# A planner's durations for GpSimd's indirect DMAs, and the order of work made anew from them

## Chip, cores and metric

The kernel runs on one core of one Trainium2 chip. The metric is the device time of one execution in microseconds, as the median of several runs. Lower is better.

## What is computed

Eight sequences of 512 tokens with 128 features pass through two macaron layers: a half-weighted mixture of experts, an attention, and the same half-weighted mixture again.

```python
x = x + 0.5 * _L0_ffn_ref(_layernorm(x, axis=-1), ...)   # 24 experts, hidden 512, top 2
x = x + _L0_attn_ref(_layernorm(x, axis=-1), ...)        # linear attention, 16 heads
x = x + 0.5 * _L0_ffn_ref(_layernorm(x, axis=-1), ...)
x = x + 0.5 * _L1_ffn_ref(_layernorm(x, axis=-1), ...)   # 8 experts, hidden 256, top 2, and a shared one
x = x + _L1_attn_ref(_layernorm(x, axis=-1), ...)        # causal attention with rotary positions
x = x + 0.5 * _L1_ffn_ref(_layernorm(x, axis=-1), ...)
```

Each mixture picks the two best experts of each token from its router's scores and adds their outputs, weighted.

## The kernel before

**Streams and rounds.** The eight sequences ("batches") are two streams `s` of four batches `b` each. There are four rounds `p` of experts: rounds 0 and 1 with the 24 experts of layer L0, rounds 2 and 3 with the 8 experts of L1. The linear attention lies at the start of round 1 and the causal attention at the start of round 3. `p` = 4 is the last combination and the store. While one stream is with its experts, the other is in routing and attention.

**The way of a round.** A batch is normalised (`norm_g`), turned into rows of two halves (`send_g`), and scored (`score`). When the batches of a part are scored, VectorE picks the experts (`r_top`), counts (`r_rank`, with a matmul on TensorE), and works out where each token's row goes (`r_slot`, lines 2216 to 2262, the last instruction of which is the cast of line 2259 that writes `slot_index`). GpSimd then writes the rows to DRAM by expert, the *scatter* (line 2520): 16 indirect DMAs for one part of a round, two batches by four tiles of 128 tokens by two choices. SyncE fetches the rows back transposed (`fetch`, line 2636). TensorE runs the experts (`l1`, lines 1711 to 1713, and `l2`, lines 1737 to 1750), ScalarE and VectorE serve them (`hid`, lines 1957 and 2065), and SyncE stores the outputs to DRAM (`ystore`, line 2649). GpSimd brings each token's two outputs back, the *gather* (line 2540): 8 indirect DMAs a batch. VectorE adds them to `x_res` (`add`, line 2332), and the next round begins. There are 16 scatters and 32 gathers, so 256 + 256 indirect DMAs.

**What sets the order.** Each engine works through its own list in order, and an instruction that waits holds back all behind it. The lists are made by `Plan` when the program is built. It is a simulation by events with a duration for each step (`work`, line 234). Whenever an engine comes free in it, `dispatch` (line 467) gives it the waiting step of lowest rank. The rank starts with 2p + s, to which `EARLIER` (line 920) adds a number by engine, kind and round in `rank_on` (line 926). A negative number puts a step ahead, a positive one back, and 2 is the distance of one round. The rank of a step of the experts on ScalarE or VectorE that has no number there is shifted by `FIRST` = -10. GpSimd has no number at all. Its list follows the rank 2p + s alone among the scatters and gathers that are ready at that moment. A scatter or a gather is not interrupted.

**Pace.** The plan's times are used once more, in `paces` (line 356). For each pair of indirect DMAs of GpSimd it looks for the last step of TensorE that has ended in the plan when that pair starts, and `keep_pace` (line 2489) makes GpSimd wait for the semaphore of this step. Before a scatter GpSimd also waits for `slot_index`, before a gather for the stores of the outputs.

Of the kernel before, what the change touches and what calls it, by code (L numbers as in the profile page):

```python
# [232 lines left out]

def work(ev):


# [680 lines left out]

EARLIER = {(SC, "bias"): 0, (SC, "ca_flip"): -1, (SC, "ca_score"): -3, (SC, "ca_v"): 3, (SC, "gates_1"): -1, (SC, "hid", 0): 0, (SC, "hid", 1): -1, (SC, "l1"): -2, (SC, "l1", 0): -1, (SC, "l1", 1): 1, (SC, "l1", 2): -1, (SC, "l1", 3): -3, (SC, "la_qk"): -3, (SC, "la_soft"): -4, (SC, "la_vg"): 3, (SC, "late_split"): -4, (SC, "norm_a"): -0.5, (SC, "norm_g", 1): 1, (SC, "norm_g", 2): 0.5, (SC, "norm_g", 3): -0.5, (SC, "r_gap"): -3, (SC, "r_gap", 1): -1, (SC, "r_soft"): 0.5, (SC, "r_soft", 2): 3, (SC, "r_soft", 3): -1, (SC, "send_a"): 2, (SC, "send_g", 1): -0.5, (SC, "send_g", 3): 2, (SC, "shared1"): -3, (SC, "shared1", 3): -0.5, (SC, "split_0"): -0.5, (SC, "split_1"): 0.5, (SC, "turn_a"): 0.5, (SC, "turn_g"): -4, (SC, "ystore"): -0.5, (SC, "ystore", 0): 1, (SC, "ystore", 2): 0.5, (PE, "ca_flip"): -1, (PE, "ca_out"): -1, (PE, "ca_q"): 0.5, (PE, "ca_score"): 2, (PE, "ca_v"): 1, (PE, "halve_0"): 2, (PE, "la_heads"): -2, (PE, "la_mix"): 0.5, (PE, "la_out"): -2, (PE, "la_qk"): -0.5, (PE, "la_vg"): -0.5, (PE, "r_end", 0): -3, (PE, "r_end", 1): -3, (PE, "r_rank"): 1, (PE, "r_rank", 0): -3, (PE, "r_rank", 1): -3, (PE, "r_rank", 2): 3, (PE, "r_rank", 3): 2, (PE, "score"): -0.5, (PE, "score", 1): 2, (PE, "score", 2): 2, (PE, "shared1"): 1, (PE, "shared2"): -4, (PE, "shared2", 3): -1, (PE, "split_0"): -3, (PE, "turn_a"): -3, (VE, "add"): 3, (VE, "add", 1): 2, (VE, "add", 2): 0.5, (VE, "bias"): 0, (VE, "ca_flip"): 0.5, (VE, "ca_k"): -3, (VE, "ca_out"): -3, (VE, "ca_score"): -3, (VE, "empties"): 2, (VE, "hid"): 0, (VE, "hid", 0): -4, (VE, "hid", 1): -3, (VE, "la_heads"): 0.5, (VE, "la_mix"): 1, (VE, "la_second"): 1, (VE, "la_soft"): -2, (VE, "norm_a", 1): -0.5, (VE, "norm_g"): -3, (VE, "norm_g", 0): 1, (VE, "norm_g", 3): -1, (VE, "r_end", 0): 3, (VE, "r_end", 2): -1, (VE, "r_end", 3): -4, (VE, "r_gap", 0): -2, (VE, "r_gap", 1): 1, (VE, "r_norm", 2): 3, (VE, "r_page", 1): 3, (VE, "r_rank"): -4, (VE, "r_rank", 0): -0.5, (VE, "r_rank", 2): -4, (VE, "r_rank", 3): 0.5, (VE, "r_send"): 3, (VE, "r_send", 1): -1, (VE, "r_share"): -1, (VE, "r_share", 1): -0.5, (VE, "r_share", 2): 3, (VE, "r_share", 3): 3, (VE, "r_slot"): -3, (VE, "r_slot", 0): 0, (VE, "r_slot", 1): 2, (VE, "r_slot", 2): 0.5, (VE, "r_soft", 3): -1, (VE, "r_top"): 1, (VE, "r_top", 0): 0.5, (VE, "r_top", 2): -1, (VE, "score"): 0.5, (VE, "score", 1): -0.5, (VE, "score", 2): 1, (VE, "score", 3): 3, (VE, "send_a"): 0, (VE, "send_g", 1): -1, (VE, "send_g", 3): 3, (VE, "shared2", 2): 2, (VE, "split_1"): -0.5}  # L920
# [1877 lines left out]
```

How the kernel before makes its waits and increments, by code:

```python
    def wait_ge(self, signal, value):  # L962
        if self.passed.get(signal, 0) < value:
            self.passed[signal] = value
            self.do.wait_ge(signal.sem, value)
# [352 lines left out]
        def second_ready(lane, layer):  # L1318
            n = LAYERS.index(layer)
            if layer.terms:
                lane.wait_ge(*w2_low.after_all(w2_halves[n]))
            else:
                lane.wait_ge(second_loaded[n], 16 * layer.chunks)
# [80 lines left out]
        def before_set(lane, ev, b):  # L1405
            pool, user = plan.sets_for(ev.p), Ev("set", ev.s, ev.p, b)
            old = pool.before[user]
            if old:
                for read in set_read(old):
                    lane.wait_ge(*read)
            elif pool.at[user] == START_SET:
                lane.wait_ge(*w1_low.after_all(w1_splits[0] + w1_splits[1]))
                for layer in LAYERS:
                    if layer.terms:
                        second_ready(lane, layer)
                for s, zeroed in enumerate(rows_zeroed):
                    lane.wait_ge(zeroed, 16 * len(ZERO_PARTS[s]))
            else:
                lane.wait_ge(block_parked, 16 * len(pieces[L1]))
# [11 lines left out]
        def gates_ready(lane, ev):  # L1431
            sent = turn_of("g", *ev[1:])
            lane.wait_ge(*w1_low.after(split_of(GATE_PART)))
            lane.wait_ge(*xt_landed[plan.xt.at[sent]].after(sent))
# [15 lines left out]
            def bank_free(ev, j=0):  # L1451
                old = plan.banks.before[ev, j]
                if old:
                    t.wait_ge(*bank_read(*old))
```

## Time and profile before

| what | value |
|---|---|
| median of 3 runs | 1012.48 us (1011.15 to 1014.36) |
| the profiled execution | 1013.01 us |
| its span, first to last instruction | 1011.7 us |
| mean granted clock of TensorE | 0.913 of full speed |
| busy: TensorE matmuls | 818.3 us, 81% |
| busy: VectorE | 658.2 us, 65% |
| busy: ScalarE | 640.2 us, 63% |
| busy: GpSimd (POOL) | 498.4 us, 49% |

The shares are averages over stages with different limits. GpSimd's busy time leaves out the 0.3 us that stand between two of its DMAs in a row, and which the views put down as "issue". TensorE's matmuls overlap, and a busy TensorE is not one at its peak.

### The profile page before, as it was taken

How to read it: one execution, taken by the hardware profiler on the slowest of the kernel's cores; microseconds unless marked ns; L12 is line 12 of the kernel's file. 1: busy time of each engine (PE TensorE's matmuls, PEld its weight loads, DVE VectorE, ACT ScalarE, POOL GpSimd, SP SyncE). 2: the span in 40 equal slices, each digit the busy share in tenths (PEclk: the TensorE clock that was granted, in tenths of full speed). 3: DMA queues.
4: the chain of work that ended last, by engine and by line, in shares of the span. 5: the costliest groups of instructions: out<-in, count | busy, mean ns of one | idle time of the engine just before them, and what ended most of it. 6: DMA issues, size and time to landing. Idle time of an engine off the chain costs nothing.

```text
span 1011.7 us, 25625 instructions
## 1 busy us (share of the span) xinstructions
PE 818.3 (81%) x9531; PEld 701.5 (69%) x9531; DVE 658.2 (65%) x2266; ACT 640.2 (63%) x1200; POOL 498.4 (49%) x519
## 2 busy tenths in 40 slices
PE   5897999998983486989898898865788979897940
PEld 3446899977883255888887798752777858686840
DVE  5986875495884784898377852588567858673022
ACT  5476789879883376888787874543566657463420
POOL 0272650370007771026374277777536637376775
PEclk9998999999997687999999999867799989998985
DMA  8888864552425124585466468542664454466852
GB/s 281 296 258 246 233 142 115 112 122 60 78 51 121 52 74 87 110 198 119 119 138 115 78 143 219 120 110 63 120 134 91 102 112 105 112 146 129 173 154 75
DMA packets 254167, 134.32 MB, mean 133 GB/s; under 512 B 171936, under 2 KB 232288, under 8 KB 254048
## 3 DMA queue, kind: packets, MB, share of 16 engines
q1 hardware_dynamic: 237664, 99.11, 42.8%
q0 software_dynamic: 16384, 33.59, 12.0%
q8 instruction: 80, 1.31, 0.6%
q14 instruction: 39, 0.32, 0.1%
HBM read 40.09 MB, written 56.89 MB: 96 GB/s over the span
## 4 chain that ended last, share of the span: by engine, by line
PE 26%; DVE 11%; POOL 8%; DMA 7%; issue 5%; ACT 4%; SPq 1%; ACTq 0%; POOLq 0%; DVEq 0%
POOL got L2540 5%; PE bank L1740 5%; POOL rows L2520 3%; PE bank L1711 3%; PE bank L1713 3%; PE bank L1712 3%; DMA got<-y_l,slot_index 2%; PE bank L1529 2%; DVE hid L2065 2%; SPq L2636 1%; DMA turned<-rows 1%; PE bank L1631 1%; PE bank L1653 1%; DMA rows<-rows_sent,slot_index 1%; PE bank L1746 1%
## 5 line engine op out<-in xcount | busy, mean ns | idle before, releaser
L2520 POOL DMA_INDIRECT rows<-rows_sent,slot_index x192 | 189.2, 985 | 303.5 <-issue 189.5
L2540 POOL DMA_INDIRECT got<-y_l,slot_index x256 | 245.6, 959 | 172.7 <-issue 68.0
L1711 PE MATMUL bank<-turned,first_high_l 128*128 128x128 f16 x1248 | 233.1, 225 | 54.2 <-DMA turned<-rows 37.3
L1712 PE MATMUL bank<-turned,first_high_l 128*128 128x128 f16 x1248 | 232.8, 224 | 0.0
L1713 PE MATMUL bank<-turned,first_low_l 128*128 128x128 f16 x1248 | 232.6, 224 | 0.0
L2065 DVE SCALAR_TENSOR_TENSOR hid<-bank,hid 128x512 f16<-128x512 f32 x220 | 145.1, 685 | 83.9 <-ACT hid L1957 82.5
L1711 PEld LDWEIGHTS bank<-turned,first_high_l 128*128 x1248 | 125.9, 101 | 64.6 <-issue 63.5
L1950 ACT ACTIVATE bank<-bank 128x512 f32<-128x512 f32 x220 | 128.0, 588 | 58.4 <-PE bank L1713 54.1
L2332 DVE SCALAR_TENSOR_TENSOR x_res<-got,share,x_res 128x128 f32<-128x128 f32 x256 | 77.6, 348 | 121.9 <-DMA got<-y_l,slot_index 119.5
L1957 ACT ACTIVATE hid<-bank 128x512 f16<-128x512 f32 x220 | 127.9, 597 | 9.3 <-PE bank L1750 5.4
L1712 PEld LDWEIGHTS bank<-turned,first_high_l 128*128 x1248 | 125.9, 101 | 4.0 <-issue 2.3
L1713 PEld LDWEIGHTS bank<-turned,first_low_l 128*128 x1248 | 126.0, 101 | 0.0
L1746 PE MATMUL bank<-second_low_l,hid 128*128 x880 | 122.7, 220 | 0.0
L1745 PE MATMUL bank<-second_high_l,hid 128*128 x880 | 122.7, 220 | 0.0
L1740 PE MATMUL bank<-second_l,hid 128*128 x736 | 115.7, 297 | 0.0
L1740 PEld LDWEIGHTS bank<-second_l,hid 128*128 128x128 f32 x736 | 101.4, 200 | 2.6 <-issue 0.6
L1968 ACT ACTIVATE y<-bank 128x512 f32<-128x512 f32 x104 | 60.9, 585 | 66.9 <-DMA y_l<-y 30.4
L1737 PE MATMUL bank<-bias,select_l 128*128 128x128 f16 x404 | 89.7, 222 | 4.5 <-ACT hid L1950 3.7
L1824 ACT ACTIVATE xn<-x_res,norm 128x128 f32<-128x128 f32 x136 | 56.0, 486 | 56.5 <-DVE norm L2103 56.4
L1745 PEld LDWEIGHTS bank<-second_high_l,hid 128*128 128x128 f16 x880 | 86.4, 98 | 2.6 <-issue 2.3
L1750 PE MATMUL bank<-second_high_l,hid 128*128 x880 | 85.6, 220 | 2.4 <-DVE hid L2065 2.4
L1746 PEld LDWEIGHTS bank<-second_low_l,hid 128*128 128x128 f16 x880 | 86.5, 98 | 0.0
(304 smaller groups left out, 1660.4 us busy)
## 6 DMA issues: line engine op xcount, KB each, us to landing
y_l<-y SPq DMA_DIRECT2D x92, 256.0 KB
rows<-own SPq DMA_DIRECT2D x14, 512.0 KB, 5.9
got<-in_w_dram SPq DMA_DIRECT2D x27, 256.0 KB, 5.0
hid<-in_w_dram SPq DMA_DIRECT2D x25, 256.0 KB, 3.9
got<-y_l,slot_index POOLq DMA_INDIRECT x256
rows<-rows_sent,slot_index POOLq DMA_INDIRECT x192, 2.2
y_l<-y SPq DMA_DIRECT2D x12, 192.0 KB
x_res<-in_x_dram SPq DMA_DIRECT2D x8, 256.0 KB, 4.8
```

Source lines behind the costliest of these rows:

```text
L1711: t.do.matmul(out, cut_of(high[c], e), xh, start=True, stop=False)
L1712: t.do.matmul(out, cut_of(high[c], e), xl, start=False, stop=False)
L1713: m = t.do.matmul(out, cut_of(low[c], e), xh, start=False, stop=True)
L1737: t.do.matmul(out, spread(select[layer][:, bass.ds(e, 1)]), bcol("b2_0" if layer is L0 else "b2_1"), start=True, stop=False)
L1740: m = t.do.matmul(out, hid[:, j * H + c * P:j * H + c * P + P], cut_of(seconds[layer][0][c], e), start=False, stop=(c == C - 1))
L1745: t.do.matmul(out, upper, cut_of(high[c], e), start=False, stop=False)
L1746: t.do.matmul(out, upper, cut_of(low[c], e), start=False, stop=False)
L1950: a.do.activation(out, hb, ACT.Gelu, scale=1 / (X_SCALE * W_SCALE)).then_inc(hidden_gelu[ev.s].sem, 1)
L1957: m = a.do.activation(hid[:, 0:n], bank_of(l1)[:, 0:n], ACT.Copy, scale=HID_SCALE)
L2065: m = v.do.scalar_tensor_tensor(hid[:, SEQ:SEQ + n], bank_of(l1)[:, 0:n], HID_SCALE, hid[:, 0:n], ALU.mult, ALU.subtract)
L2520: d = g.do.indirect_dma_start(rows_dram[s], at, rows[:, 2 * D * i:2 * D * i + 2 * D], None)
L2540: d = g.do.indirect_dma_start(got_mem[slot][:, col:col + D], None, y_dram[layer][s][layer.team(ev.i)], at)
```

## The change

Two durations of `work` are raised, those of the scatter and the gather. `EARLIER` is replaced as a whole. Nothing else is edited: no instruction is added or taken away, and what follows is another order of the instructions in the engines' lists and other steps for GpSimd to wait for. `EARLIER` is one line of some 150 entries. Here it stands with the entries of which the text speaks, one group to a line.

```diff
-        "scatter": [[(GP, 1.0 * TOP_K * tokens, 2.2)]], "gather": [[(GP, 1.0 * TOP_K * BT, 2.4)]], "add": [[(VE, 3.0, 0.1)]],
+        "scatter": [[(GP, 1.265 * TOP_K * tokens, 2.2)]], "gather": [[(GP, 1.23 * TOP_K * BT, 2.4)]], "add": [[(VE, 3.0, 0.1)]],
...
-EARLIER = {
-  (SC, "hid", 0): 0, (SC, "hid", 1): -1, (SC, "ystore"): -0.5, (SC, "ystore", 0): 1, (SC, "ystore", 2): 0.5,
-  (PE, "score"): -0.5, (PE, "score", 1): 2, (PE, "score", 2): 2,
-  (VE, "add"): 3, (VE, "add", 1): 2, (VE, "add", 2): 0.5,
-  (VE, "hid"): 0, (VE, "hid", 0): -4, (VE, "hid", 1): -3,
-  (VE, "norm_g"): -3, (VE, "norm_g", 0): 1, (VE, "norm_g", 3): -1,
-  (VE, "r_top"): 1, (VE, "r_top", 0): 0.5, (VE, "r_top", 2): -1,
+EARLIER = {
+  (SC, "hid"): 1, (SC, "hid", 0): 0.5, (SC, "ystore", 0): 2, (SC, "ystore", 1): 1, (SC, "ystore", 2): 0.5,
+  (PE, "score"): 0, (PE, "score", 2): -4,
+  (VE, "add", 1): -2, (VE, "add", 2): -1, (VE, "add", 3): 0.5,
+  (VE, "hid", 0): -2,
+  (VE, "norm_g"): 3, (VE, "norm_g", 0): -2, (VE, "norm_g", 2): -1, (VE, "norm_g", 3): -0.5,
+  (VE, "r_top"): -2, (VE, "r_top", 0): -0.5, (VE, "r_top", 1): -1, (VE, "r_top", 3): -1,
...
```

## Rows read from the trace of the kernel before

**Rows 1.** Page, busy us, share of the span, number of instructions of TensorE and GpSimd

```profile
PE 818.3 (81%) x9531; PEld 701.5 (69%) x9531; DVE 658.2 (65%) x2266; ACT 640.2 (63%) x1200; POOL 498.4 (49%) x519
```

**Rows 2.** Page, the chain that ended last, its shares of the span by line

```profile
POOL got L2540 5%; PE bank L1740 5%; POOL rows L2520 3%; PE bank L1711 3%; PE bank L1713 3%; PE bank L1712 3%; DMA got<-y_l,slot_index 2%; PE bank L1529 2%; DVE hid L2065 2%; SPq L2636 1%; DMA turned<-rows 1%; PE bank L1631 1%; PE bank L1653 1%; DMA rows<-rows_sent,slot_index 1%; PE bank L1746 1%
```

**Rows 3.** Windows: stretch, its length, busy us (instructions) by engine, clock, DMA, GB/s

```profile
302.00:385.00 83.00, 43.85 (x337) 31.57 (x337) 57.19 (x208) 41.26 (x69) 63.48 (x64) 0.75 0.31 78
...
574.00:717.00 143.00, 110.87 (x1214) 95.99 (x1214) 84.41 (x332) 71.53 (x138) 108.53 (x112) 0.84 0.56 132
...
881.00:1007.00 126.00, 82.03 (x919) 76.86 (x918) 43.91 (x179) 44.55 (x86) 92.05 (x96) 0.86 0.59 135
...
970.00:980.00 10.00, 3.15 (x29) 2.90 (x27) 2.46 (x8) 1.09 (x2) 7.56 (x9) 0.91 0.47 131
```

**Rows 4.** Groups by line on GpSimd, with busy us, mean ns, idle before, releasers

```profile
L2540 POOL DMA_INDIRECT got<-y_l,slot_index x256 | 245.6, 959 | 172.7 <-issue 68.0 <-PE bank L1750 35.8 <-PE bank L1500 18.3
L2520 POOL DMA_INDIRECT rows<-rows_sent,slot_index x192 | 189.2, 985 | 303.5 <-issue 189.5 <-PE bank L1713 45.9 <-PE bank L1462 40.5
```

**Rows 5.** GpSimd in order of time: start, us, instruction, idle before and its releaser

```profile
362.91 0.94 POOL L2540 DMA_INDIRECT got<-y_l,slot_index  x1 [0.31 <-issue]
364.16 1.00 POOL L2520 DMA_INDIRECT rows<-rows_sent,slot_index  x1 [0.30 <-issue]
...
686.22 1.00 POOL L2520 DMA_INDIRECT rows<-rows_sent,slot_index  x1 [0.30 <-issue]
...
844.96 1.00 POOL L2520 DMA_INDIRECT rows<-rows_sent,slot_sent  x1 [0.30 <-issue]
...
901.11 1.00 POOL L2520 DMA_INDIRECT rows<-rows_sent,slot_index  x1 [0.30 <-issue]
```

**Rows 6.** Chain that ended last, pieces of four scatters: start, us, what

```profile
372.65 0.96 POOL rows L2520
373.91 0.96 POOL rows L2520
...
704.23 0.95 POOL rows L2520
...
862.03 0.96 POOL rows L2520
...
911.64 0.95 POOL rows L2520
```

**Rows 7.** VectorE in order of time, the last cast of four `r_slot`

```profile
357.08 0.40 DVE L2259 CAST slot_index<-route_l 128x8 int32<-128x8 f32 x1
...
679.32 0.17 DVE L2259 CAST slot_index<-route_l 128x8 int32<-128x8 f32 x1
...
835.29 0.16 DVE L2259 CAST slot_index<-route_l 128x8 int32<-128x8 f32 x1
...
896.40 0.17 DVE L2259 CAST slot_index<-route_l 128x8 int32<-128x8 f32 x1
```

**Rows 8.** Waits over the span: who waited for whom, us, times, longest

```profile
DVE x_res L2332 <- DMA got<-y_l,slot_index: 119.5, 28, 31.5
```

**Rows 9.** VectorE in order of time around 330 us

```profile
329.79 1.26 DVE L2332 SCALAR_TENSOR_TENSOR x_res<-got,share,x_res 128x128 f32<-128x128 f32 x4 [6.60 <-DMA got<-y_l,slot_index]
334.75 1.26 DVE L2332 SCALAR_TENSOR_TENSOR x_res<-got,share,x_res 128x128 f32<-128x128 f32 x4 [3.70 <-DMA got<-y_l,slot_index]
335.94 0.25 DVE L2139 TENSOR_SCALAR scores<-bank 128x96 f32<-128x96 f32 x1
```

**Rows 10.** GpSimd in order of time, two waits for TensorE

```profile
471.32 0.96 POOL L2520 DMA_INDIRECT rows<-rows_sent,slot_index  x1 [2.98 <-PE bank L1713]
...
931.25 0.96 POOL L2520 DMA_INDIRECT rows<-rows_sent,slot_sent  x1 [4.21 <-PE bank L1713]
```

**Rows 11.** GpSimd and VectorE in order of time around 305 us

```profile
304.95 1.71 POOL L2520 DMA_INDIRECT rows<-rows_sent,slot_index  x1 [0.30 <-issue]
...
304.83 1.12 DVE L2370 SCALAR_TENSOR_TENSOR first_high_l<-first_low_l,set_small,first_low_l 128x512 f32<-128x512 f32 x1
```

More of the change, by code:

```diff
@@ L916 @@
 EXPERT_STAGES = ("regs", "fetch", "l1", "hid", "l2", "ystore")
-EARLIER = {(SC, "bias"): 0, (SC, "ca_flip"): -1, (SC, "ca_score"): -3, (SC, "ca_v"): 3, (SC, "gates_1"): -1, (SC, "hid", 0): 0, (SC, "hid", 1): -1, (SC, "l1"): -2, (SC, "l1", 0): -1, (SC, "l1", 1): 1, (SC, "l1", 2): -1, (SC, "l1", 3): -3, (SC, "la_qk"): -3, (SC, "la_soft"): -4, (SC, "la_vg"): 3, (SC, "late_split"): -4, (SC, "norm_a"): -0.5, (SC, "norm_g", 1): 1, (SC, "norm_g", 2): 0.5, (SC, "norm_g", 3): -0.5, (SC, "r_gap"): -3, (SC, "r_gap", 1): -1, (SC, "r_soft"): 0.5, (SC, "r_soft", 2): 3, (SC, "r_soft", 3): -1, (SC, "send_a"): 2, (SC, "send_g", 1): -0.5, (SC, "send_g", 3): 2, (SC, "shared1"): -3, (SC, "shared1", 3): -0.5, (SC, "split_0"): -0.5, (SC, "split_1"): 0.5, (SC, "turn_a"): 0.5, (SC, "turn_g"): -4, (SC, "ystore"): -0.5, (SC, "ystore", 0): 1, (SC, "ystore", 2): 0.5, (PE, "ca_flip"): -1, (PE, "ca_out"): -1, (PE, "ca_q"): 0.5, (PE, "ca_score"): 2, (PE, "ca_v"): 1, (PE, "halve_0"): 2, (PE, "la_heads"): -2, (PE, "la_mix"): 0.5, (PE, "la_out"): -2, (PE, "la_qk"): -0.5, (PE, "la_vg"): -0.5, (PE, "r_end", 0): -3, (PE, "r_end", 1): -3, (PE, "r_rank"): 1, (PE, "r_rank", 0): -3, (PE, "r_rank", 1): -3, (PE, "r_rank", 2): 3, (PE, "r_rank", 3): 2, (PE, "score"): -0.5, (PE, "score", 1): 2, (PE, "score", 2): 2, (PE, "shared1"): 1, (PE, "shared2"): -4, (PE, "shared2", 3): -1, (PE, "split_0"): -3, (PE, "turn_a"): -3, (VE, "add"): 3, (VE, "add", 1): 2, (VE, "add", 2): 0.5, (VE, "bias"): 0, (VE, "ca_flip"): 0.5, (VE, "ca_k"): -3, (VE, "ca_out"): -3, (VE, "ca_score"): -3, (VE, "empties"): 2, (VE, "hid"): 0, (VE, "hid", 0): -4, (VE, "hid", 1): -3, (VE, "la_heads"): 0.5, (VE, "la_mix"): 1, (VE, "la_second"): 1, (VE, "la_soft"): -2, (VE, "norm_a", 1): -0.5, (VE, "norm_g"): -3, (VE, "norm_g", 0): 1, (VE, "norm_g", 3): -1, (VE, "r_end", 0): 3, (VE, "r_end", 2): -1, (VE, "r_end", 3): -4, (VE, "r_gap", 0): -2, (VE, "r_gap", 1): 1, (VE, "r_norm", 2): 3, (VE, "r_page", 1): 3, (VE, "r_rank"): -4, (VE, "r_rank", 0): -0.5, (VE, "r_rank", 2): -4, (VE, "r_rank", 3): 0.5, (VE, "r_send"): 3, (VE, "r_send", 1): -1, (VE, "r_share"): -1, (VE, "r_share", 1): -0.5, (VE, "r_share", 2): 3, (VE, "r_share", 3): 3, (VE, "r_slot"): -3, (VE, "r_slot", 0): 0, (VE, "r_slot", 1): 2, (VE, "r_slot", 2): 0.5, (VE, "r_soft", 3): -1, (VE, "r_top"): 1, (VE, "r_top", 0): 0.5, (VE, "r_top", 2): -1, (VE, "score"): 0.5, (VE, "score", 1): -0.5, (VE, "score", 2): 1, (VE, "score", 3): 3, (VE, "send_a"): 0, (VE, "send_g", 1): -1, (VE, "send_g", 3): 3, (VE, "shared2", 2): 2, (VE, "split_1"): -0.5}
@@ new lines @@
+EARLIER = {(SC, "ca_flip"): -3, (SC, "ca_score"): 1, (SC, "gates_1"): 3, (SC, "halve_0"): 2, (SC, "hid"): 1, (SC, "hid", 0): 0.5, (SC, "l1"): 1, (SC, "l1", 1): -1, (SC, "l1", 3): 2, (SC, "la_qk"): -0.5, (SC, "la_vg"): 3, (SC, "late_split"): -4, (SC, "norm_a"): 2, (SC, "norm_a", 1): 2, (SC, "norm_a", 3): -4, (SC, "norm_g"): 2, (SC, "norm_g", 1): 2, (SC, "norm_g", 2): 2, (SC, "norm_g", 3): 1, (SC, "r_gap"): -4, (SC, "r_soft", 3): -2, (SC, "send_a"): 1, (SC, "send_g"): -4, (SC, "send_g", 1): 3, (SC, "send_g", 2): -1, (SC, "send_g", 3): 1, (SC, "shared1"): 3, (SC, "shared1", 3): -4, (SC, "split_0"): -4, (SC, "turn_g"): -4, (SC, "ystore", 0): 2, (SC, "ystore", 1): 1, (SC, "ystore", 2): 0.5, (PE, "ca_out"): 0.5, (PE, "ca_q"): -0.5, (PE, "halve_0"): 2, (PE, "la_heads"): -3, (PE, "la_out"): -2, (PE, "r_end"): 2, (PE, "r_end", 0): -3, (PE, "r_end", 2): 1, (PE, "r_rank"): -2, (PE, "r_rank", 0): -2, (PE, "r_rank", 1): -0.5, (PE, "r_rank", 2): 0, (PE, "r_rank", 3): 1, (PE, "score"): 0, (PE, "score", 2): -4, (PE, "shared1"): 1, (PE, "shared1", 2): 1, (PE, "shared2", 3): -1, (PE, "split_1"): 0, (PE, "turn_a"): 2, (VE, "add", 1): -2, (VE, "add", 2): -1, (VE, "add", 3): 0.5, (VE, "ca_flip"): -2, (VE, "ca_k"): -2, (VE, "ca_out"): 1, (VE, "ca_score"): -3, (VE, "gates_1"): 0.5, (VE, "hid", 0): -2, (VE, "la_heads"): -2, (VE, "la_mix"): -0.5, (VE, "la_second"): -0.5, (VE, "la_soft"): -2, (VE, "late_split"): 0, (VE, "norm_a"): -0.5, (VE, "norm_a", 1): -1, (VE, "norm_a", 3): 3, (VE, "norm_g"): 3, (VE, "norm_g", 0): -2, (VE, "norm_g", 2): -1, (VE, "norm_g", 3): -0.5, (VE, "r_end", 1): 2, (VE, "r_end", 2): 0, (VE, "r_end", 3): 1, (VE, "r_gap"): -4, (VE, "r_gap", 0): -3, (VE, "r_gap", 1): -3, (VE, "r_norm"): -3, (VE, "r_norm", 2): 1, (VE, "r_page", 1): 3, (VE, "r_rank"): -3, (VE, "r_rank", 3): -3, (VE, "r_send", 1): -0.5, (VE, "r_send", 2): 2, (VE, "r_send", 3): 0, (VE, "r_share", 0): 1, (VE, "r_share", 2): 2, (VE, "r_share", 3): 3, (VE, "r_slot", 0): -0.5, (VE, "r_slot", 1): 2, (VE, "r_slot", 2): 1, (VE, "r_soft"): 0.5, (VE, "r_top"): -2, (VE, "r_top", 0): -0.5, (VE, "r_top", 1): -1, (VE, "r_top", 3): -1, (VE, "score", 2): 2, (VE, "score", 3): -0.5, (VE, "selects"): 1, (VE, "send_a"): 0, (VE, "send_g"): 2, (VE, "send_g", 1): -4, (VE, "send_g", 3): -2, (VE, "shared2", 2): -1, (VE, "shared2", 3): -1, (VE, "split_0"): -4, (VE, "turn_g"): 3}
```

## The prediction

> **What bounds the kernel now.** I read the page first. TensorE is busy for 81% of the span and GpSimd for 49% [rows 1], so neither is the bound everywhere. In the chain that ended last the two lines of GpSimd's indirect DMAs together have 8% and no line of TensorE more than 5% [rows 2]. The chain goes from engine to engine, and the order in the lists decides much of its length. The windows then show where GpSimd is the bound. In three blocks it runs without a pause: 64 DMAs in 83 us, 112 in 143 us and 96 in 126 us, while TensorE is busy for 44, 111 and 82 us and its mean clock lies at 0.75, 0.84 and 0.86 of full speed [rows 3]. So 272 of the 512 DMAs run where GpSimd is saturated, and TensorE is idle there for 39 + 32 + 44 = 115 us.
>
> Next I read the pitch. An indirect DMA counts 959 or 985 ns of busy time [rows 4], but the next one starts 1.26 us later in a scatter [rows 6] and 1.25 us later in a gather [rows 5], as 0.3 us of "issue" stand between them. The plan counted 1.0 us. The new figures, 1.265 and 1.23, are right within 2%. The old plan saw the blocks as 64, 112 and 96 us, some 20% too short, and believed GpSimd free where it was not.
>
> **The change, part by part.** *Durations.* No DMA becomes shorter: 512 instructions at the same pitch, 0 us. What changes is which step stands where. By the new figures a scatter counts 16 x 1.265 = 20.2 us instead of 16, a gather 8 x 1.23 = 9.8 instead of 8.
>
> *GpSimd's list.* A scatter releases a round of experts, so how long it stands ready and isn't started can be read. `r_slot`'s last cast ends at 357.48, 679.49, 835.45 and 896.57 [rows 7]. The scatters that need it start at 364.16, 686.22, 844.96 and 901.11 [rows 5]. In each case a gather stands in front, and the delays are 6.7, 6.7, 9.5 and 4.5 us, together 27.4 us. All four scatters have pieces in the chain that ended last [rows 6], so the delay is on the path. It is the gain if every scatter goes first. But a gather that is overtaken lands a whole scatter, 20.2 us, later, and its batch is the start of the next round. How many of the four are turned round can't be read from the diff, since GpSimd's list has no number of its own and comes out of when the steps are ready in the plan. I take half, 13.7 us, with 0 and 27.4 as the ends.
>
> *VectorE's list.* In all it waits 119.5 us for gathered rows [rows 8]. Where it waits, others stand behind it. Around 330 us the two halves of an `add` wait 6.60 and 3.70 us, and a `score` comes directly behind [rows 9], on which `r_top`, `r_rank`, `r_slot` and the late scatter at 364 depend. In the plan an `add` enters the list only when its gather has landed, and with 8 us for a gather it was put in too early. With 9.8 us it goes behind what is ready. Against this, the new numbers put `add` of round 1 four places forward (2 to -2) and that of round 3 from 3 to 0.5. The most to be had at this place is what the `score` could be earlier, 335.94 - 329.79 = 6.2 us [rows 9]. It pays only if the scatter behind it can use it, so it is largely the same time as the 6.7 us above. I count 0, and 6 as the upper bound.
>
> *The tail.* TensorE is busy for only 3.15 us between 970 and 980 [rows 3] and ends there. At 1006.5 GpSimd's last DMA ends, some 30 us later. The 16 gathers of the last team (two batches) need the last outputs: 16 x 1.25 = 20 us. So up to 10 us of backlog could go if the gathers of the teams that end earlier are done by then. This too is earned only if the third block begins earlier. I count 0 and put 8 into the lower end.
>
> *ScalarE's and TensorE's lists.* `hid` and `ystore` on ScalarE go back by 0.5 to 2 places, `hid` on VectorE in rounds 0 and 1 goes from -4 and -3 to -2 and -10, `score` of round 2 on TensorE from 2 to -4, `norm_g` of round 1 on VectorE from -3 to 3. I see no single wait in the trace that these remove. As a whole they are the orders that suit the new durations. I count 0 with 4 us on either side: no row excludes a gain or a loss, and 4 us is the size of the single waits in rows 9 and 10.
>
> *Pace.* A change in the plan's durations also moves the steps of TensorE that GpSimd waits for. In the old plan pair n of a gather or scatter stood at 2.0 n, now at 2.46 n or 2.53 n, and at the end of a block of 48 pairs the step named stands over 22 us later in the plan. Before, GpSimd was slower than the plan, so the step was mostly long past (0.30 us of idle [rows 5]). The two waits of size were 2.98 and 4.21 us [rows 10]. Now this cushion is gone, and if TensorE is late against the plan, GpSimd is held with all that stands behind it. I take 2 us, between 0 and the price of the third rival below.
>
> *DMA length.* At 304.95 one DMA takes 1.71 instead of 0.96 us, while VectorE works for 1.12 us on a gate with both inputs in SBUF [rows 11]. Against the usual 0.94 to 0.96 us, the means [rows 4] leave at most 8 us over all 512 DMAs, and another order moves a fraction of that: 0, within 2 either way. The Trainium skill (SBUF — State Buffer, Who interferes with whom) says that VectorE and GpSimd lock each other out of a shared pair of ports, and that an instruction of VectorE with two SBUF inputs contends with GpSimd's reads. The trace agrees at this place.
>
> *Sum.* 13.7 - 2 = 11.7 us less. The profiled execution took 1013.01 us (span 1011.7 and 1.3 around it), half a microsecond above the median of 1012.48. From the profiled execution the sum gives 1001.3 and from the median 1000.8. **I predict 1001 us.**
>
> One rule speaks against the new durations. The Trainium skill (DMA: Bandwidth & Descriptors, Latency and other measured facts) puts the first-byte latency of a DMA that GpSimd issues at about 1 us, and calls it the overhead of making the descriptors. If that were the pitch, the old 1.0 would be right, and the new plan would count 512 x 0.25 = 128 us too much on GpSimd. The trace decides otherwise.
>
> **The rivals.** *First: the order is nearly worth nothing* (1010 to 1015). Every scatter pulled forward delays a gather, and both streams meet at the end. For it: the gathers are in the chain more than the scatters [rows 2], so a delayed gather costs as well. Against it: TensorE is idle for 115 us in the blocks [rows 3], so the present exchange isn't balanced. Time: 13.7 gained and 13.7 lost, 1012.
>
> *Second: a larger gain* (below 990). All four scatters start at once (27.4) and the shorter third block takes part of the backlog (8): 1012.5 - 35.4 = 977. For it: the plan erred by 20% on the engine that was saturated in a third of the span. Against it: the four exchanges influence one another, and later blocks shift.
>
> *Third, slower: the pace.* In the three blocks the clock stood at 0.75, 0.84 and 0.86 [rows 3]. With the busy times of 44, 111 and 82 us, TensorE lost 44 x 0.25 + 111 x 0.16 + 82 x 0.14 = 40 us there against full clock. If the plan counts TensorE's steps at full clock, GpSimd now waits for steps that come late, where it had 14 to 24 us of cushion (20% of each block). If a third of the 40 us is passed on and the order brings nothing, the time is 1012.5 + 13 = 1025. It decides from the point where TensorE's lag in a block is larger than what the scatters gain, 13.7 us. For it: the 4.21 us at 931 [rows 10] lie in a scatter of the third block, right on the path. Against it: the clock is low where TensorE waits for GpSimd, so its steps are few there and mostly done in time.
>
> *Fourth: the new plan is right by itself but the chip's other errors grow* (transposes, stores, the queue of SyncE), which a new order meets anew. It works like the third with a smaller price and is counted with it.
>
> **How the numbers follow.** The forecast's case, 990 to 1009: 0.45. The second rival: 0.16. The first: 0.14. The third and fourth: 0.25. A difference of over 0.3% (3 us) is about what a measurement of this kernel can tell from no change. Faster by more is 0.45 + 0.16, and with the edge of the first rival 0.62. Within it 0.12, slower 0.26. The range reaches from 983 (the second rival without its last 6 us) to 1023 (the third nearly whole). The forecast's own range is 990 to 1009.
>
> **What would show it.** Right: GpSimd's scatters start within 2 us of the last cast of `r_slot`, VectorE's waits for gathered rows fall well below 119.5 us, and GpSimd's three blocks begin earlier or are broken up. GpSimd's busy time must stay at 498 us within 3 us. For the third rival: GpSimd's idle time before its DMAs shows waits for TensorE of 2 us and more inside the blocks. For the first: the delays at the scatters are gone, but as much idle time of VectorE or TensorE stands before the adds. Wrong altogether would be a gain or loss before 300 us, where GpSimd is not saturated: then the orders on ScalarE, VectorE and TensorE decide, and the durations are only the occasion.

## The result, and the profile after

The changed kernel takes 963.97 us (median of 4 runs, 960.89 to 970.6), the kernel before 1012.35 beside it. The ratio is 0.953, with an interval of 0.948 to 0.958: 4.7% faster, where I had forecast 1.1%. The direction was right. The time lies outside both ranges that I had given (990 to 1009, and 983 to 1023 with the rivals). The profiled execution took 960.89 us, with a span of 959.5.

The page first: its busy line, two of the lines in 40 slices (tenths busy on GpSimd, tenths of full clock on TensorE), the chain that ended last, and the groups of GpSimd's two kinds of DMA.

```profile
span 959.5 us, 25612 instructions
...
PE 810.3 (84%) x9531; PEld 689.7 (72%) x9531; DVE 659.8 (69%) x2266; ACT 638.6 (67%) x1200; POOL 495.6 (52%) x519
...
POOL 0076441173003777042557077777764675577775
PEclk9898999999998686899999999997999999999985
...
PE 15%; DVE 10%; POOL 7%; DMA 5%; issue 5%; ACT 3%; SPq 0%; ACTq 0%; POOLq 0%; DVEq 0%
POOL got L2540 4%; PE bank L1740 4%; POOL rows L2520 3%; PE bank L1529 2%; DMA xt<-rows_sent 2%; DMA got<-y_l,slot_index 2%; PE bank L1711 1%; DVE x_res L2332 1%; PE bank L1713 1%; PE bank L1712 1%; DVE norm L2078 1%; PE bank L1631 1%; DMA turned<-rows 1%; PE bank L1653 1%; DVE x_res L2415 1%
```

```profile
L2540 POOL DMA_INDIRECT got<-y_l,slot_index x256 | 245.6, 959 | 230.4 <-PE bank L1610 73.1
L2520 POOL DMA_INDIRECT rows<-rows_sent,slot_index x192 | 187.4, 976 | 199.9 <-issue 110.6
```

No engine is given less to do: GpSimd is busy for 495.6 us (498.4 in [rows 1]), and its DMAs take 959 and 976 ns (959 and 985 in [rows 4]). The chain is as mixed as before, with the two lines of GpSimd at 7% in place of 8% [rows 2]. So most of the 52 us lie between the instructions.

To see where, I cut each span at the last `ystore` of each expert stage. TensorE's work is then nearly the same on either side of a cut, apart from some 50 matmuls. VectorE's is not, as the second cut shows below. These are the second, third and last two stretches of before (start and end, length, busy us and instructions of PE, PEld, DVE, ACT and POOL, clock, DMA share, GB/s):

```profile
184.30:311.30 127.00, 116.87 (x1572) 104.35 (x1569) 93.88 (x282) 106.92 (x194) 37.59 (x39) 0.97 0.43 91
311.30:498.40 187.10, 134.53 (x1714) 116.30 (x1715) 128.68 (x415) 119.70 (x214) 87.32 (x90) 0.86 0.47 106
...
931.00:974.00 43.00, 39.47 (x470) 38.23 (x467) 4.95 (x16) 19.54 (x36) 32.63 (x34) 1.00 0.82 184
974.00:1011.70 37.70, 0.00 (x0) 0.00 (x0) 9.83 (x32) 0.49 (x1) 24.58 (x26) 0.56 0.33 88
```

And the same four of after:

```profile
180.50:296.80 116.30, 111.82 (x1554) 99.51 (x1551) 75.42 (x206) 101.04 (x184) 30.46 (x32) 1.00 0.40 88
296.80:482.10 185.30, 146.44 (x1774) 123.80 (x1775) 149.54 (x493) 127.50 (x228) 92.86 (x96) 0.85 0.50 114
...
876.10:922.80 46.70, 42.86 (x506) 42.00 (x506) 5.55 (x19) 20.21 (x36) 35.42 (x38) 0.96 0.87 197
922.80:959.50 36.70, 0.00 (x0) 0.00 (x0) 9.20 (x30) 0.49 (x1) 23.88 (x26) 0.55 0.32 88
```

The same reading for all eleven stretches, where idle is the length less TensorE's busy time:

| stretch ends with | length before | after | TensorE idle before | after |
|---|---|---|---|---|
| round 0, stream 0 | 184.3 | 180.5 | 23.6 | 22.2 |
| round 0, stream 1 | 127.0 | 116.3 | 10.1 | 4.5 |
| round 1, stream 0 | 187.1 | 185.3 | 52.6 | 38.9 |
| round 1, stream 1 | 106.6 | 100.1 | 8.7 | 6.0 |
| round 2, stream 0 | 60.1 | 55.0 | 7.6 | 7.2 |
| round 2, stream 1, first team | 93.3 | 87.4 | 27.1 | 21.2 |
| round 2, stream 1, second team | 52.5 | 46.0 | 2.9 | 1.3 |
| round 3, stream 0, first team | 61.6 | 56.4 | 9.8 | 4.5 |
| round 3, stream 0, second team | 58.5 | 49.1 | 9.9 | 3.0 |
| round 3, stream 1 | 43.0 | 46.7 | 3.5 | 3.8 |
| tail | 37.7 | 36.7 | 37.7 | 36.7 |

TensorE's idle time falls from 193 to 149 us, which is 44 of the 52 us. The other 8 are shorter busy time (818.3 to 810.3), beside a mean granted clock over the span of 0.931 in place of 0.913. There is no one place. Nine stretches give 2 to 11 us each, the last expert stage gives 4 back and the tail gives 1. 14.5 us are there by the second cut (311.3 against 296.8), and in that stretch of before GpSimd is busy for 38 of 127 us. Not all of the 14.5 us is won there. By this cut TensorE is 7 us short of its work of before (51 matmuls) and VectorE 19 us, and the third stretch makes it up: it is hardly shorter, but holds 12 us more of TensorE and 21 us more of VectorE. What is won by the second cut is TensorE's idle time, 33.7 us before and 26.7 after.

What GpSimd does is seen best in order of time, around its first block (start, us, instruction, idle before it and its releaser):

```profile
300.50 0.94 POOL L2540 DMA_INDIRECT got<-y_l,slot_index  x1 [73.08 <-PE bank L1610]
...
304.94 0.94 POOL L2540 DMA_INDIRECT got<-y_l,slot_index  x1 [2.25 <-PE bank L1602]
...
329.45 0.95 POOL L2540 DMA_INDIRECT got<-y_l,slot_index  x1 [2.12 <-PE bank L1557]
...
333.20 0.95 POOL L2540 DMA_INDIRECT got<-y_l,slot_index  x1 [0.30 <-issue]
334.45 1.49 POOL L2520 DMA_INDIRECT rows<-rows_sent,slot_index  x1 [0.30 <-issue]
...
364.29 0.95 POOL L2540 DMA_INDIRECT got<-y_l,slot_index  x1 [0.30 <-issue]
365.54 1.08 POOL L2520 DMA_INDIRECT rows<-rows_sent,slot_index  x1 [0.30 <-issue]
```

The last casts of `r_slot` ahead of these two scatters, and of two more, in VectorE's order of time:

```profile
325.67 0.41 DVE L2259 CAST slot_index<-route_l 128x8 int32<-128x8 f32 x1
...
359.31 0.17 DVE L2259 CAST slot_index<-route_l 128x8 int32<-128x8 f32 x1
...
650.97 0.17 DVE L2259 CAST slot_index<-route_l 128x8 int32<-128x8 f32 x1
...
850.04 0.17 DVE L2259 CAST slot_index<-route_l 128x8 int32<-128x8 f32 x1
```

```profile
654.07 1.00 POOL L2520 DMA_INDIRECT rows<-rows_sent,slot_index  x1 [0.30 <-issue]
...
852.81 1.00 POOL L2520 DMA_INDIRECT rows<-rows_sent,slot_index  x1 [0.30 <-issue]
```

Scatters still stand ready behind gathers. The one at 334.45 waits 8.4 us from the end of its cast (326.08). The four of [rows 5] and [rows 7] go from 6.7, 6.7, 9.5 and 4.5 us to 6.1, 2.9, 1.2 and 2.6. But summed over all sixteen scatters the time from the last cast of `r_slot` to the first DMA is 66.1 us before and 66.2 after. Of this 23.8 and 30.2 us lie in round 0, where there is no gather to stand behind, so rounds 1 to 3 have 42.3 and 36.0. What moved is when they are ready: the casts of [rows 7] at 679 and 896 stand at 651 and 850. So less waiting gives at most 6 us; for the rest, everything ahead of the scatters is earlier.

Which pairs were turned round needs no trace: `Plan`, run on either kernel, gives the lists. Among the 48 scatters and gathers of GpSimd two places differ. The first scatter of round 1 (stream 0) stands behind three gathers of stream 1 and no longer ahead of them. In round 2 the two scatters of stream 1 each pass one gather. Of the four pairs of [rows 5] only one is turned round by this, that of the scatter at 686 (6.7 to 2.9 us). The other three stand behind the same gather as before. The other lists differ far more: TensorE's at 616 of 941 places, ScalarE's at 554 of 885, VectorE's at 472 of 631. The first DMA of GpSimd at which its list differs is this one of before, so up to 302 us the two kernels have the same order on GpSimd:

```profile
302.30 1.00 POOL L2520 DMA_INDIRECT rows<-rows_sent,slot_index  x1 [72.95 <-issue]
```

Waits of after over the span (who waited for whom, us, times, longest):

```profile
DVE x_res L2332 <- DMA got<-y_l,slot_index: 87.7, 22, 29.4
...
PE bank L1711 <- DMA turned<-rows: 5.5, 3, 2.9
```

VectorE waits 87.7 us for gathered rows instead of 119.5 [rows 8]. TensorE waits 5.5 us for rows turned by a transfer. Before this line read:

```profile
PE bank L1711 <- DMA turned<-rows: 37.3, 6, 13.3
```

### The profile page after: what moved, and what is told of

The parts are those of the page before. It is cut to its first block and busy times, and to the rows that moved or that the text cites. A ratio compares the mean times of both kernels' runs of the same rounds, so it can differ in the third digit from the quotient of the medians.

```text
span 959.5 us, 25612 instructions
## 1 busy us (share of the span) xinstructions
PE 810.3 (84%) x9531; PEld 689.7 (72%) x9531; DVE 659.8 (69%) x2266; ACT 638.6 (67%) x1200; POOL 495.6 (52%) x519
## 5 line engine op out<-in xcount | busy, mean ns | idle before, releaser
L1711 PE MATMUL bank<-turned,first_high_l 128*128 128x128 f16 x1248 | 224.8, 220 | 23.9 <-DVE hid L2065 9.1
L1712 PE MATMUL bank<-turned,first_high_l 128*128 128x128 f16 x1248 | 224.4, 220 | 0.0
L1713 PE MATMUL bank<-turned,first_low_l 128*128 128x128 f16 x1248 | 224.3, 220 | 0.0
L1711 PEld LDWEIGHTS bank<-turned,first_high_l 128*128 x1248 | 122.9, 99 | 32.6 <-issue 32.0
L2332 DVE SCALAR_TENSOR_TENSOR x_res<-got,share,x_res 128x128 f32<-128x128 f32 x256 | 77.1, 348 | 94.8 <-DMA got<-y_l,slot_index 87.7
L1712 PEld LDWEIGHTS bank<-turned,first_high_l 128*128 x1248 | 122.9, 98 | 2.1 <-issue 1.0
L1713 PEld LDWEIGHTS bank<-turned,first_low_l 128*128 x1248 | 122.8, 98 | 0.0
L1740 PE MATMUL bank<-second_l,hid 128*128 x736 | 112.4, 291 | 0.0
L1740 PEld LDWEIGHTS bank<-second_l,hid 128*128 128x128 f32 x736 | 98.4, 195 | 2.4 <-issue 0.3
L1950 ACT ACTIVATE hid<-bank 128x512 f32<-128x512 f32 x96 | 53.9, 581 | 54.6 <-PE bank L1713 52.7
```

Of the source, the lines that this page charges most:

```text
L1711: t.do.matmul(out, cut_of(high[c], e), xh, start=True, stop=False)
L1712: t.do.matmul(out, cut_of(high[c], e), xl, start=False, stop=False)
L1713: m = t.do.matmul(out, cut_of(low[c], e), xh, start=False, stop=True)
L1740: m = t.do.matmul(out, hid[:, j * H + c * P:j * H + c * P + P], cut_of(seconds[layer][0][c], e), start=False, stop=(c == C - 1))
L1950: a.do.activation(out, hb, ACT.Gelu, scale=1 / (X_SCALE * W_SCALE)).then_inc(hidden_gelu[ev.s].sem, 1)
```

## The experiments

**How they are built.** All kernels below carry one edit more. Each of SyncE's 136 transposing transfers is replaced by three plain ones that move the same bytes in pieces of 256 bytes to the same place, so the values computed from there on are not the reference's. Lists, waits and instructions of the engines stay. Line numbers are one higher than in after (ten higher where four pairs are named, below).

```diff
+MOVES = [(0, 0, 4), (1, 0, 2), (1, 2, 4)]
...
+            def move_plain(dst, src, landed):
+                for h, lo, hi in MOVES:
+                    y.do.dma_start(dst[:, h, lo:hi, :], src[:, h, lo:hi, :]).then_inc(landed.sem, 16)
...
-                y.do.dma_start_transpose(dst, rows_of(ev).bitcast(F16)).then_inc(xt_landed[slot].sem, 16)
+                move_plain(dst.rearrange("p (h t) k -> p h t k", h=2), rows_of(ev).bitcast(F16).rearrange("p (t h k) -> p h t k", h=2, k=P), xt_landed[slot])
```

Three theories are to be told apart; the texts of the single runs add a few of their own. **A, the fit:** the ranks suit one exact set of durations, the durations must be those of the chip, and only both together give the gain, everywhere in the list. **B, the scatters:** the gain is the order of scatters and gathers on GpSimd, the main term of my sum. **C, the ranks:** the new table is simply better, and the durations are only the occasion.

**Both halves alone.** `before` and `after` with plain transfers as a base, then only the durations, then only the ranks. The diffs of the last two:

```diff
-        "scatter": [[(GP, 1.0 * TOP_K * tokens, 2.2)]], "gather": [[(GP, 1.0 * TOP_K * BT, 2.4)]]
+        "scatter": [[(GP, 1.265 * TOP_K * tokens, 2.2)]], "gather": [[(GP, 1.23 * TOP_K * BT, 2.4)]]
```

```diff
-EARLIER = {(SC, "bias"): 0, (SC, "ca_flip"): -1, ...
+EARLIER = {(SC, "ca_flip"): -3, (SC, "ca_score"): 1, ...
```

> The kernel before, with each of the 136 transposing transfers of SyncE replaced by three plain ones of the same bytes in the same 256-byte pieces, into the same place and waited for by the same instructions. The rows arrive untransposed, so the values from there on are others; instructions, lists and waits are the same. All theories: the same as the kernel before within 2%. It is the base for the runs that follow.

> The kernel after with the same plain transfers (other values from there on). If the gain has nothing to do with the transposes, its ratio to the kernel before is 0.94 to 0.965. If it is less than half as large, the transposes carry it.

> Plain transfers (other values), the new durations with the ranks of before. Theory A (the ranks are fitted to one exact set of durations, and are no better than chance with any other): the plan's own end rises from 949 to 1063, and the chip takes 3 to 6% more than the kernel before. Theory B (the gain comes from the plan knowing when GpSimd is free, whatever the ranks): 1 to 5% less than the kernel before.

> Plain transfers (other values), the old durations with the ranks of after. Theory A: the plan's own end is 1039, and GpSimd's DMAs are longer on the chip than in this plan, so 3 to 8% more than the kernel before. Theory C (the new ranks are simply better, with any durations): 3 to 5% less than the kernel before.

The plan has an end of its own, the end of its last step by its own durations, which the kernel's planner works out while the kernel is built. The table has it beside what the chip took (us; ratio to the kernel before in the same runs, with its interval):

| kernel | durations | ranks | plan's end | chip | chip less plan | ratio |
|---|---|---|---|---|---|---|
| p_before | old | old | 949.3 | 1012.17 | +63 | 1.003 (1.000 to 1.005) |
| p_durations | new | old | 1063.2 | 1035.89 | -27 | 1.030 (1.024 to 1.035) |
| p_ranks | old | new | 1038.9 | 1096.97 | +58 | 1.090 (1.085 to 1.095) |
| p_after | new | new | 973.9 | 965.83 | -8 | 0.959 (0.954 to 0.963) |

The base holds: plain transfers leave before within 0.3% and keep 4.1 of the 4.7%. Either half alone loses, 3.0% and 9.0% (for the second A had allowed 8%). C falls with p_ranks. B isn't settled by these and has a run of its own below. The column of differences says why. With the old durations the plan believes in an end that the chip misses by some 60 us. With the new ones the chip ends 8 to 27 us before the plan does. The old error is of the size of the DMAs in the saturated blocks: 272 [rows 3] at 0.26 us each is 71 us (an estimate from the pitch of [rows 5] and the plan's 1.0). So the ranks of before were good in a plan that the chip doesn't follow.

The waits of p_ranks show how the wrong pair looks: VectorE's adds and TensorE both stand before transfers that the plan believed landed. The first two rows are p_ranks, the two behind them p_after (who waited for whom, us, times, longest).

```profile
DVE x_res L2333 <- DMA got<-y_l,slot_index: 173.2, 38, 26.4
...
PE bank L1712 <- DMA turned<-rows: 68.4, 6, 23.2
```

```profile
DVE x_res L2333 <- DMA got<-y_l,slot_index: 91.1, 25, 27.4
...
PE bank L1712 <- DMA turned<-rows: 4.9, 4, 2.7
```

VectorE's waits alone don't tell the kernels apart: p_durations has 89.1 us of them, as few as p_after, and loses 3%. TensorE's waits for turned rows do go with the time in these runs, 33.5 us in p_durations and 36.9 in p_before, where p_after has 4.9.

**Other ranks, found independently.** Is it this table, or the durations? I searched ranks at random from an empty table, with the plan's own end as the only measure, once with the new durations and once with the old. The tables have nothing of after's or before's. A few entries:

```diff
 # new durations, third table
+EARLIER = {(SC, "hid"): 3, (SC, "hid", 0): -3, (SC, "hid", 1): -4, (SC, "ystore"): -2, (PE, "score"): -3, (VE, "add", 2): 3, (VE, "hid"): -4, (VE, "r_top"): -4, ...
 # old durations, fourth table
+EARLIER = {(SC, "hid"): -2, (SC, "ystore"): 0, (PE, "score", 0): 3, (VE, "add", 2): 0.5, (VE, "hid"): 0.5, (VE, "r_top"): -1, ...
```

> Plain transfers (other values from there on). The new durations and a third set of ranks, found by an independent random search from an empty table until its plan ended at 974.3, as the plan of after does (973.9). Theory A (a list made and tuned with GpSimd's durations right keeps on the chip what it has in the plan): 0.955 to 0.975 of the kernel before. Theory E (after is one lucky draw among plans that look alike): anywhere from 0.96 to 1.02.

> Plain transfers (other values). The old durations and a fourth set of ranks, from the same kind of search with the old durations, until its plan ended at 953.9 (before: 949.3). Theory A: the plan errs where GpSimd is saturated and the chip pays for it, 0.99 to 1.04 of the kernel before. Theory F (any fresh search gives the gain, the durations are beside the point): 0.95 to 0.98.

With the new durations: plan 974.3, chip 958.2, ratio 0.949 (0.944 to 0.954). With the old: plan 953.9, chip 1017.08, ratio 1.008 (1.005 to 1.010). The first reproduces the gain (a little more of it than the 0.955 to 0.975 of A) with ranks that differ from after's in sign: -2 instead of 2 for `ystore` of round 0, and on ScalarE -3 and -4 instead of 0.5 and 1 for `hid` of rounds 0 and 1. The second has a plan 20 us shorter and is 59 us slower on the chip. So a fresh search alone gave nothing. With one table of each kind, the plan that was searched decided, and not which table came out. The waits tell the same. The first two rows are the search with new durations, the last two the one with old:

```profile
DVE x_res L2333 <- DMA got<-y_l,slot_index: 83.8, 22, 26.7
...
PE bank L1712 <- DMA turned<-rows: 5.6, 3, 3.6
```

```profile
DVE x_res L2333 <- DMA got<-y_l,slot_index: 113.4, 31, 29.7
...
PE bank L1712 <- DMA turned<-rows: 26.5, 7, 8.2
```

One form of B stays open here. `Plan` gives p_new_search and after the very same list for GpSimd, all 48 scatters and gathers, though TensorE's lists differ at 466 of 941 places. The kernels that gain nothing (p_before, p_durations, p_ranks, p_old_search, and p_gather_125_b below) each have another. No run has this order of GpSimd with the other lists of before, so it is not excluded that much of the gain lies in it. Not all can: up to 302 us GpSimd's lists are the same in before and after, and TensorE's idle time is already 7 of the 44 us lower.

**One duration, by 0.02 us.** If the fit is as exact as A says, an error far below what the chip could show by itself must undo the gain. Ranks and all else are those of p_after.

```diff
-"gather": [[(GP, 1.23 * TOP_K * BT, 2.4)]]
+"gather": [[(GP, 1.25 * TOP_K * BT, 2.4)]]
```

> Plain transfers (other values). The kernel after with 1.25 for the gather's duration instead of 1.23, which is nearer to the trace, with its ranks kept. Theory A (ranks fit one exact set of durations, and a change of 0.02 us throws other orders): the plan's own end rises from 974 to 1041 and the chip takes 1010 to 1050. Theory B (what counts is that the durations are about right): 955 to 975.

1018.6 us, ratio 1.008 (1.005 to 1.010): the whole gain is gone, and 52.8 us against p_after. The plan's own end goes from 973.9 to 1041.5. A gather of the plan lasts 0.16 us more, all 32 together 5 us, and the plan grows by 68. `Plan` alone shows how narrow the fit is: with the same ranks it ends at 1008.6 with 1.22 and at 1040.0 with 1.24, neither of which was run on a chip. The new length is no worse than the old (the pitch is 1.25 us [rows 5]). The ranks no longer suit it: TensorE's list differs from that of p_after at 546 of 941 places and GpSimd's at 10 of 48. My reading, which no run takes apart, is that ranks decide among steps that are ready within fractions of a microsecond of one another, and where one such choice goes the other way, all that follows shifts.

**The scatters first.** This is my main term by itself. In GpSimd's list of before the four scatters of [rows 5] change places with the gather directly ahead. All other lists stay. The waits of the pace are left out here, as they would name steps of the old order, so it is compared with p_before_no_pace (1001.41, below).

```diff
+SCATTERS_FIRST = [(Ev("gather", 1, 1, 3), Ev("scatter", 0, 1, 1)), (Ev("gather", 0, 3, 2), Ev("scatter", 1, 2, 0)),
+                  (Ev("gather", 1, 3, 3), Ev("scatter", 0, 3, 1)), (Ev("gather", 0, 4, 1), Ev("scatter", 1, 3, 0))]
...
+        for later, first in SCATTERS_FIRST:
+            line = self.order[GP]
+            n = line.index(later)
+            line[n:n + 2] = [first, later]
```

> Plain transfers (other values from there on), no pace. The kernel before without the pace, and in GpSimd's list alone the four scatters that stood ready behind a gather (1,1,3; 0,3,2; 1,3,3; 0,4,1) put ahead of it. By the prediction's main term 0 to 27 us less than the kernel before without pace (1001 us), 13.7 in the middle: 974 to 1001. Theory A (the gain lies in the order of the other lists, and a scatter that goes first only takes from the gather): 996 to 1006.

1054.13 us, 53 us slower instead of up to 27 faster, and beyond what either theory had allowed. VectorE in order of time shows the price at three of the four places:

```profile
381.59 1.26 DVE L2342 SCALAR_TENSOR_TENSOR x_res<-got,share,x_res 128x128 f32<-128x128 f32 x4 [20.24 <-DMA got<-y_l,slot_index]
...
872.96 1.27 DVE L2342 SCALAR_TENSOR_TENSOR x_res<-got,share,x_res 128x128 f32<-128x128 f32 x4 [16.11 <-DMA got<-y_l,slot_index]
...
946.95 1.26 DVE L2342 SCALAR_TENSOR_TENSOR x_res<-got,share,x_res 128x128 f32<-128x128 f32 x4 [21.77 <-DMA got<-y_l,slot_index]
```

```profile
DVE x_res L2342 <- DMA got<-y_l,slot_index: 189.6, 34, 26.7
```

The gather that is overtaken lands a scatter later, as I had worked out (20.2 us). But its `add` stands at a fixed place in VectorE's list, and all of VectorE waits with it. Together it waits 189.6 us, where without the exchange it is 107.0. What a plan gives that may move the adds along is not this run, and three of its four exchanges are not in after at all. In after, which may, the four scatters gain 15 us of their 27, though only one of them by an exchange (3.8 us). Two others lose 16: the first of round 1 (0.9 to 8.4 us) and the last of round 2 (0.9 to 9.3).

**The pace.** Without the waits of `keep_pace`, for before, after, and the ranks of the search with new durations:

```diff
-                step = paces[ev, pair]
+                step = None
```

> Plain transfers (other values). The kernel before without GpSimd's waits for steps of TensorE, every list as it was. Theory A (the order of the lists decides, and the pace was slack before): within 0.8% of the plain before, 1012. Theory D (the pace keeps GpSimd's transfers from meeting others): slower by over 1%.

> Plain transfers (other values). The kernel after without GpSimd's waits for steps of TensorE, every list as it was. Theory A: 960 to 970 us beside the plain after's 966. Theory D (the gain comes from a pace that now fits): 985 us or more. The prediction's rival that the pace costs time: 950 to 959.

> Plain transfers (other values). The lists of the independent search with the new durations (958 us), without GpSimd's waits for steps of TensorE. The pace cost 9 us in the kernel before and 5 in the one after, so 948 to 956.

1001.41 us, 960.7 and 952.15, ratios 0.990 (0.987 to 0.994), 0.951 (0.949 to 0.954) and 0.942 (0.937 to 0.946). The pace costs 11 us with the old lists and some 5 and 6 with the two new ones, the last of these within the intervals. For the kernel before this is over what A had allowed (0.8%). In the traces of p_before and p_before_no_pace the first DMA of the first block starts at 302.8 and 297.8 us, so nearly half of the 11 us is lost before it. For the lists of after the two traces can't say as much: the profiled execution without the pace took 964.45 us, only 1 us less than the one with it. The third kernel is the fastest of all: 0.942 where p_after has 0.959 and the changed kernel 0.953. It has only been timed with plain transfers.

**Runs that settle little.** The kernels of p_gather_125_b, p_scatters_first_b and p_new_search_no_pace_b had run before on another chip, under the same names without the last letter, and plain_after_9, which is p_after under another name, on a third. The kernel before itself took 1195 and 1214 us there, so of these only the ratios can be read.

> The kernel after with each of the 136 transposing transfers of SyncE replaced by three plain ones of the same bytes in the same 256-byte pieces, into the same place (the values from there on are others). If the gain has nothing to do with the transposes, 950 to 975 us. If it is less than half as large, the transposes carry it.

It came to 1138.57 us against 1213.91, 0.938 from one run of each. p_gather_125 came to 1176.28 against 1195.04 (0.988), p_scatters_first to 1426.75 (1.196) and p_new_search_no_pace to 1415.25 (1.187). The last section returns to them.

## Why the prediction was wrong in size

**The views and the pitch: right.** The old plan was too short by 20% on GpSimd, and the pitch is 1.25 and 1.26 us in both traces. The Trainium skill (DMA: Bandwidth & Descriptors, Latency and other measured facts) gives about 1 us of first-byte latency for a DMA that GpSimd issues. I had weighed this as a possible pitch, and it would have made the new durations the wrong ones. As a pitch the traces contradict it, and the plans made with the new durations end within 8 to 27 us of the chip, the others some 60 off.

**Late scatters, 13.7 us: the step that failed.** I read four pieces of lateness off the trace and put them down as time to be won. I took half of the four pairs as turned round, and `Plan` turns one. Alone the exchange of all four costs 53 us, and in after the sum over all scatters is the same 66 us (6 us less in rounds 1 to 3). Of the four, one starts within 2 us of its cast, as I had asked of all. A step that stands ready and isn't started was not a loss by itself here. My reading is that it would have been one if what stood ahead of it hadn't been needed as soon. I had written this down as the first rival, and gave it a price of nothing, because I let the gathers lose what the scatters won. With VectorE's list fixed they lost far more. That the forecast had the right sign is luck, as its main term, tried alone, is a loss.

**VectorE's, ScalarE's and TensorE's lists, 0 within 4: the term that was too small.** I looked for single waits in the trace that the new ranks would remove, found none, and set them at 0 with 4 us on either side. I also misread the table: `ystore` of round 3 on ScalarE doesn't go back but forward, from -0.5 to -10. The stretches show 44 us less idle time of TensorE, from 0.4 to 14 us in each but one. 7 of the 44 are won before the first block of GpSimd, where its order is the same, and that is beyond my 4 us. The other 37 can't be divided between these lists and GpSimd's. They also show the sign that I had named for "wrong altogether", a gain before 300 us. But the conclusion I had tied to it, that the durations are then only the occasion, is wrong as well: with the old durations the same ranks cost 9%. The premise that hid this was that orders bring single waits. They bring the fit of a whole table (117 numbers before, 110 after, not the 150 that I had said) to the plan, and I could read its worth only as a whole. The plan's ends were there before the result: 949.3 for the old, with the chip 63 us behind, and 973.9 for the new. A plan that the chip follows would have put the new kernel near 974, where it took 964. That was the better forecast.

**VectorE's waits for gathered rows: mechanism right.** They fell well below 119.5 us, to 87.7. Before the last two stretches they went from 48 to 25 us. But p_durations has as few (89.1) and is slower, so the fall is no gain by itself.

**The tail, 0 and at most 8: right.** Measured by the cuts: 37.7 and 36.7 us.

**Pace, 2 us lost: wrong in sign, and in size for before.** Waits of 2 us and more inside the blocks are there as the third rival wanted (2.25 and 2.12 above, 1.93 at 623 us), but the large ones of [rows 10] are gone, and the cost of all falls from 11 to 5 us. Why the pace costs less in the new plan wasn't tried. The cushion of the third rival was misfigured as well: 20% of the three blocks are 17 to 29 us, not 14 to 24.

**DMA length, 0 within 2: right.** 192 scatters by 9 ns are 1.7 us.

**The clock.** I had given none of the gain to it. TensorE's busy time is 8 us shorter at a higher mean clock (0.931, before 0.913). Whether the clock follows from the smaller idle time or adds to the gain, no run here tells.

**The chances.** The second rival had the right sign and 977 us as its end. Even with all four scatters and the backlog it could not reach 964, since its terms were those of GpSimd alone.

## What to carry to other kernels

Where a planner lays out the lists, compare its own end with the chip's time before anything else. Here the chip was 6% behind the plan, and 5% was won once the duration of one saturated engine was its pitch and the ranks were made anew. Change durations and ranks only together, since here a correct duration with the old ranks cost 3%, and 0.02 us on one duration undid everything. Run the planner on both kernels and compare the lists before you count what an exchange is worth. A wait that stands in a trace of fixed lists is not a gain until the steps behind it on the other engines have been moved as well.

## What the runs showed of the hardware that I had not expected

Two chips ran all kernels slower: the kernel before took 1195 and 1214 us there, where the others took 1009 to 1012. The busy times of VectorE, ScalarE and GpSimd are nearly the same there, and TensorE's is longer: 943.6 us at a mean clock of 0.79 in the kernel below, where its twin has 811.4 at 0.936. The two kernels with the pace came out 2% better against before than elsewhere (0.988 and 0.938, elsewhere 1.008 and 0.959). The two without it came out far worse: 1.196 and 1.187, elsewhere 1.042 and 0.942. The page and the waits of the 1415 us kernel, whose twin took 952:

```profile
PE 943.6 (67%) x9531; PEld 764.3 (54%) x9531; DVE 659.6 (47%) x2266; ACT 640.8 (45%) x1199; POOL 492.6 (35%) x519
```

```profile
POOL got L2541 <- DMA y_l<-y: 337.8, 9, 80.0
...
ACT bank L1951 <- remote: 154.3, 21, 14.4
...
ACT hid L1951 <- remote: 138.9, 17, 24.7
```

ScalarE has 293 us of idle time whose releaser the profile names "remote", in pieces of up to 25 us, and such rows do not stand in its twin. GpSimd's indirect DMAs keep their pitch of 1.25 us in a block (around 300 us). What "remote" stands for, and whether the pace protects against it or the two without it suffered for another reason, stays open. It was not tried further: before without the pace has no run on such a chip.
